# Attention and expert block on one core: normalising the head outputs without transposing them, and row maxima by transposing VectorE reductions

## What is computed

```python
s = jnp.einsum('bthd,bshd->bhts', q, k) * scale
logits = DEG * jnp.log(jnp.abs(s) + 1e-30) + log_G[:, :, :, None] - log_G[:, :, None, :]   # DEG = 2
logits = jnp.where(mask, logits, -jnp.inf)                        # causal
m = jax.lax.stop_gradient(jnp.max(logits, axis=-1, keepdims=True))
a = jnp.exp(logits - m)
num = jnp.einsum('bhts,bshd->bthd', a, v)
den = jnp.sum(a, axis=-1).transpose(0, 2, 1)
y = num / (den[..., None] + 1e-06)
mu = jnp.mean(y, axis=-1, keepdims=True)
var = jnp.mean((y - mu) ** 2, axis=-1, keepdims=True)
y = (y - mu) / jnp.sqrt(var + 1e-09) * ln_w
return y.reshape(B, T, hq * d) @ w_proj
```

## Time and profile before

| | |
|---|---|
| time, median of three runs | 1030.43 us (1028.33 to 1031.97) |
| profiled execution, first to last instruction | 1027.0 us |
| busy: PE, DVE, ACT, POOL | 959.8, 876.1, 676.7, 631.0 us |
| attention pairs | the first scores begin at 148 us, the last nt copy is at 992 us |

### The profile page before, as it was taken

One profiled execution on the slowest core, in us unless ns is written; L12 is line 12 of the kernel. 1 busy time (PEld: TensorE's weight loads), 2 busy tenths in 40 slices (PEclk: granted clock), 3 DMA queues, 4 the chain that ended last, 5 costly groups with the idle time before them and its releaser, 6 DMA issues.

```text
span 1027.0 us, 23345 instructions
## 1 busy us (share of the span) xinstructions
PE 959.8 (93%) x8871; PEld 707.3 (69%) x8871; DVE 876.1 (85%) x1730; ACT 676.7 (66%) x1077; POOL 631.0 (61%) x593
## 2 busy tenths in 40 slices
PE   3999989899999999999999999999999999999964
PEld 2675567567676767687777677777768677768643
DVE  5668738899999998998999898988898989898892
ACT  1243447676766677868778867787876877886731
POOL 0320438889898966666658566748575856766711
PEclk9999999999999999999999999999999999999996
DMA  9401105443434354454444344435434535433540
GB/s 262 102 1 47 51 12 146 106 107 95 108 98 101 101 135 111 104 135 119 104 126 124 97 126 107 119 82 143 104 98 118 127 85 133 112 97 96 147 125 22
DMA packets 77952, 108.66 MB, mean 106 GB/s; under 512 B 15853, under 2 KB 46445, under 8 KB 77712
## 3 DMA queue, kind: packets, MB, share of 16 engines
q1 hardware_dynamic: 72768, 104.50, 39.3%
q0 software_dynamic: 5072, 2.67, 1.9%
HBM read 31.61 MB, written 11.36 MB: 42 GB/s over the span
## 4 chain that ended last, share of the span: by engine, by line
PE 72%; DVE 16%; POOL 4%; issue 4%; ACT 2%; DMA 1%; SPq 1%; POOLq 0%; DVEq 0%; ACTq 0%
PE PS L545 19%; PE PS L737 19%; PE PS L770 18%; PE PS L540 6%; DVE PS L1336 3%; PE PS L588 3%; PE PS L591 3%; PE PS L598 3%; DVE U L1336 2%; DVE PS L1329 2%; POOL U L1439 1%; DVE SM L1361 1%; DVE U L1300 1%; POOL xe_d L1471 1%; PE PS L561 1%
## 5 line engine op out<-in xcount | busy, mean ns | idle before, releaser
L737 PE MATMUL PS<-Qt,Kt 64*128 64x256 f32 (+1 forms) x2560 | 276.8, 366 | 13.5 <-POOL Qt L1442 9.4
L737 PEld LDWEIGHTS PS<-Qt,Kt 64*128 64x128 f32 x2560 | 229.7, 188 | 52.9 <-POOL Qt L1442 11.3
L916 ACT ACTIVATE U<-PS 128x1024 f32<-128x1024 f32 x144 | 140.9, 1023 | 62.5 <-PE PS L737 58.7
L1439 POOL TENSOR_TENSOR U<-U,consts 128x512 f32<-128x512 f32 x96 | 126.2, 1315 | 45.5 <-DMA U<-U 45.5
L770 PE MATMUL PS<-U 128*64 128x256 f32 (+1 forms) x1344 | 139.8, 349 | 0.2 <-ACT U L912 0.2
L1461 POOL TENSOR_SCALAR_AFFINE_SELECT U<-U 128x256 f32<-128x256 f32 x128 | 61.8, 560 | 102.9 <-ACT U L841 102.6
L770 PEld LDWEIGHTS PS<-U 128*64 128x64 f32 x1344 | 93.2, 137 | 40.2 <-issue 5.7
L1507 POOL TENSOR_TENSOR U<-U,SM 128x1024 f32<-128x1024 f32 x32 | 72.2, 2257 | 68.0 <-DVE SM L1356 68.0
L1336 DVE SCALAR_TENSOR_TENSOR PS<-U,ES,PS 128x512 f32<-128x512 f32 x144 | 108.4, 752 | 4.7
L1300 DVE SCALAR_TENSOR_TENSOR U<-PS,U 128x768 f32<-128x768 f32 x96 | 88.3, 952 | 26.2 <-PE PS L737 23.9
L841 ACT ACTIVATE U<-U,negG 128x256 f32<-128x256 f32 (+1 forms) x256 | 98.7, 455 | 5.6 <-DMA U<-H_d 5.3
(11 more groups left out here) (177 smaller groups left out, 1890.7 us busy)
## 6 DMA issues: line engine op xcount, KB each, us to landing
G<-U SPq DMA_DIRECT2D x512, 64.0 KB
U<-U SPq DMA_DIRECT2D x192, 128.0 KB
U<-H_d SPq DMA_DIRECT2D x32, 512.0 KB
Kt<-Kt SPq DMA_DIRECT2D x32, 256.0 KB, 3.9
U<-in_w SPq DMA_DIRECT2D x21, 256.0 KB
acc<-in_x SPq DMA_DIRECT2D x4, 512.0 KB, 5.5
ye_d<-G SPq DMA_DIRECT2D x4, 512.0 KB, 8.0
U<-ye_d SPq DMA_DIRECT2D x4, 512.0 KB, 5.3
```

Of the source, the lines that this page charges most:

```text
L737: mm = te.matmul(bank[:, 256 * n:256 * n + 256 - lo], Kt[u % 2][(ki + hd) % 2][rows, 128 * j:128 * j + 128], Qt[p % 2][m // 2][rows, 256 * ...
L916: s.activation(A[n % NA], PS[:, first:first + 1024], ACT.Square, scale=0.125, bias=GUARD).then_inc(a_so, 1)
L1439: g.tensor_tensor(sw, sw, sinT[:, cols], ALU.mult).then_inc(made, 1)
```

## The change

It does two things, and moves what hangs on them.

Row maxima: once `RUN` is written, DVE itself reduces it with `apply_transpose`: from 128 x 512 it makes 16 columns of `MR`, in each group of 32 partitions the maximum over the partitions of that group. SP moves 16 columns (2 KB a DMA) rather than 512, into `MF`, still 16 DMAs a pair. `fold` on `G`, the four `max` flips and the reduction at L1255 go. `RUN` is one buffer rather than two.

Norm: the values stay as they are, channels on partitions. ACT copies the sums directly into `Y` (four buffers rather than two) and squares the whole into `SQ` (`sq`). Once for two pairs, TensorE multiplies a 128 x 32 selection matrix with `SQ` (`ss`: eight matmuls with 256 columns, each into 32 PSUM partitions), which gives the sums of squares and the squared denominators; DVE (`scales`) transposes them in 32 x 32 blocks, forms the factors of both pairs in 14 small operations on 32 to 64 columns, and transposes back. SP stores the factors in DRAM (`roots`, one DMA of 128 KB) and reads them back spread over partitions (`spread`, four DMAs that each write 64 partitions x 4 KB, one for each head of each pair), into `SQ`. POOL multiplies `Y` by it (`norm`, once a pair, 128 x 1024), and `wp` takes `Y` as it is. All `y` and `fin` flips, the copies L871 and L877, `sums`, `variance`, `root`, `n1` and `n2` go. The jobs get new ticks; `wp` moves from 59.3 to 62, its addition from 49.5 and 54.2 to 63.6 and 64.

Two constants, GUARD and CLAMP, are changed, and the selection matrix is added to the constants. Core of the diff:

```diff
-GUARD = 1e-15
-CLAMP = 60.0
+GUARD = 1e-8
+CLAMP = 30.0
+FLOOR = 1e-17
...
-PE_AT = [(34.43, "max", 0), (19.9, "y", 0), (23.88, "y", 1), (51.85, "fin", 0), (58.3, "fin", 1), (59.31, "wp", 0),
-         (59.72, "wp", 1), (1.41, "xe", 0), (10.46, "up", 0), (14.9, "up", 1), (15.75, "up", 2), (32.48, "up", 3),
+PE_AT = [(33, "ss", 0), (62, "wp", 0), (62.1, "wp", 1), (1.41, "xe", 0), (10.46, "up", 0), (14.9, "up", 1), (15.75, "up", 2), (32.48, "up", 3),
...
-          (10.31, "decay", 3), (23.4, "y", 0), (31.69, "y", 1), (54.54, "fin", 0), (55.63, "fin", 1),
-          (43.3, "ysq", 0), (8.58, "xe", 0), (21.82, "up", 0), (23.77, "up", 1), (25.18, "up", 2), (44.23, "up", 3),
+          (10.31, "decay", 3), (36, "sq", 0), (29, "sq", 1), (8.58, "xe", 0), (21.82, "up", 0), (23.77, "up", 1), (25.18, "up", 2), (44.23, "up", 3),
...
-DVE_AT = [(23.72, "fold", 0), (27.44, "max", 0), (49.5, "wp", 0), (54.22, "wp", 1), (27.9, "sum", 0),
-          (32.03, "var", 0), (34, "root", 0), (34.29, "root", 1), (37.4, "root", 2), (28.36, "up", 4),
+DVE_AT = [(33, "scales", 0), (63.6, "wp", 0), (64, "wp", 1), (28.36, "up", 4),
...
-           (3.66, "vs", 3), (30.16, "n1", 0), (38.34, "n2", 0), (-21.4, "k", 0), (-15.9, "k", 1), (-15.66, "q", 0),
+           (3.66, "vs", 3), (67, "norm", 0), (51, "norm", 1), (-21.4, "k", 0), (-15.9, "k", 1), (-15.66, "q", 0),
...
+         (-25.73, "swapq", 0), (-11.27, "keys", 0), (-14.53, "row", 0), (-10.6, "weights", 0), (4.79, "weights", 1), (32, "roots", 0), (34.5, "spread", 0)]
...
-        RUN = [take(512) for _ in range(2)]
+        RUN = take(512)
         D = [take(384) for _ in range(3)]
-        Y = [take(1024) for _ in range(2)]
-        YT = [take(1024) for _ in range(2)]
-        NT, VS0 = take(512), take(384)
+        Y = [take(1024) for _ in range(4)]
+        ZT, RT, RR, MF = (take(256) for _ in range(4))
+        VS0 = take(384)
...
             def rows(p, w):
 
-                m = ORDER[w]
-                sp.wait_ge(s_zy, 64)
-                sp.wait_ge(v_mx, 16 * p + MAXOPS[w + 1])
-                if p:
-                    sp.wait_ge(v_fold, 2 * p)
+                m, u, c = ORDER[w], p // 2, 16 * (4 * (p % 4) + w)
+                sp.wait_ge(v_red, 4 * p + w + 1)
+                if u > 1:
+                    sp.wait_ge(v_m, u - 1)
                 for j in range(4):
-                    sy.dma_start(G[32 * m:32 * m + 32, 512 * j:512 * j + 512],
-                                 RUN[w % 2][32 * j:32 * j + 32]).then_inc(s_g[w % 2], 16)
+                    o = 128 * (u % 2) + 64 * (p % 2) + 16 * j
+                    sy.dma_start(MF[32 * m:32 * m + 32, o:o + 16],
+                                 MR[32 * j:32 * j + 32, c:c + 16]).then_inc(s_g[u % 2], 16)
+
+            def store_roots(u):
+
+                sp.wait_ge(v_rr, u + 1)
+                if u > 1:
+                    sp.wait_ge(s_rb[0], 32 * (u - 1))
+                    sp.wait_ge(s_rb[1], 32 * (u - 1))
+                sy.dma_start(R_d[128 * (u % 2):128 * (u % 2) + 128], RR).then_inc(s_rd, 16)
+
+            def spread_roots(u):
+
+                sp.wait_ge(s_rd, 16 * (u + 1))
+                sp.wait_ge(p_ss, u + 1)
+                for i in range(2):
+                    for hd in range(2):
+                        sy.dma_start(SQ[i][64 * hd:64 * hd + 64, :].rearrange("p (m q) -> p m q", m=4),
+                                     R_v[u % 2, 2 * i + hd].partition_broadcast(64)).then_inc(s_rb[i], 16)
...
-                elif kind == "max":
-                    p = job[1]
+                elif kind == "ss":
+                    u = job[1]
                     pb = bank_of(job)
-                    pe.wait_ge(v_fold, 2 * p + 2)
-                    for k2 in range(2):
-                        for hd in range(2):
-                            q, o = 2 * k2 + hd, 256 * hd + 128 * k2
-                            tr = flip(pb[:, 128 * q:128 * q + 128], F[:, o:o + 128])
-                    tr.then_inc(p_max, 1)
-                elif kind == "y":
-                    p, i = job[1:]
-                    pb = bank_of(job)
-                    pe.wait_ge(a_nt, 2 * p + i + 1)
-                    for q in range(4):
-                        tr = flip(pb[:, 128 * q:128 * q + 128], NT[:, 128 * q:128 * q + 128])
-                    tr.then_inc(p_y, 1)
-                elif kind == "fin":
-                    p, half = job[1:]
-                    pb = bank_of(job)
-                    pe.wait_ge(g_n2, p + 1)
-                    for q in range(4):
-                        o = 512 * half + 128 * q
-                        tr = flip(pb[:, 128 * q:128 * q + 128], Y[p % 2][:, o:o + 128])
-                    tr.then_inc(p_fin, 1)
+                    pe.wait_ge(a_sq, 2 * u + 2)
+                    pe.wait_ge(s_ct, 16)
+                    for i in range(2):
+                        for m in range(4):
+                            mm = te.matmul(pb[32 * m:32 * m + 32, 0:256], K_[:, C_SEL + 32 * i:C_SEL + 32 * i + 32],
+                                           SQ[i][:, 256 * m:256 * m + 256], start=i == 0, stop=i == 1)
+                    mm.then_inc(p_ss, 1)
                 elif kind == "wp":
                     u, half = job[1:]
                     h = 2 * u % 8
                     pb = bank_of(job)
-                    pe.wait_ge(a_yt, 4 * u + 4)
+                    pe.wait_ge(g_n, 2 * u + 2)
                     for q in range(4):
                         o = 512 * half + 128 * q
                         for pp in range(2):
-                            mm = product(pb[:, 128 * q:128 * q + 128], YT[pp][:, o:o + 128],
+                            mm = product(pb[:, 128 * q:128 * q + 128], Y[(2 * u + pp) % 4][:, o:o + 128],
...
-                elif kind == "y":
-                    p, i = job[1:]
-                    ac.wait_ge(p_y, 2 * p + i + 1)
-                    if p > 1:
-                        ac.wait_ge(p_fin, 2 * (p - 2) + 2)
-                    s.activation(Y[p % 2].rearrange("p (m w c) -> p w m c", m=2, w=2)[:, i],
-                                 P[BANK[job]].rearrange("p (m c) -> p m c", m=2), ACT.Copy).then_inc(a_y, 1)
-                elif kind == "fin":
-                    p, half = job[1:]
-                    ac.wait_ge(p_fin, 2 * p + half + 1)
-                    ac.wait_ge(v_f, 15 * p + 3)
-                    s.activation(YT[p % 2][:, 512 * half:512 * half + 512], P[BANK[job]][:, :], ACT.Copy).then_inc(a_yt, 1)
...
-                    ac.wait_ge(p_y, 2 * p + i)
-                    s.activation(NT, P[4][:, :], ACT.Copy).then_inc(a_nt, 1)
+                    if p > 3:
+                        ac.wait_ge(p_wp, 2 * (p // 2 - 1))
+                    s.activation(Y[p % 4].rearrange("p (m w c) -> p w m c", m=2, w=2)[:, i],
+                                 P[4][:, :].rearrange("p (m c) -> p m c", m=2), ACT.Copy).then_inc(a_nt, 1)
...
-                elif kind == "ysq":
-                    ac.wait_ge(g_n1, p + 1)
-                    ac.wait_ge(p_wp, 2 * (p // 2))
-                    s.activation(YT[p % 2][:, 0:1008].rearrange("p (n d) -> p n d", d=63),
-                                 Y[p % 2].rearrange("p (n d) -> p n d", d=64)[:, :, 0:63], ACT.Square).then_inc(a_ysq, 1)
+                elif kind == "sq":
+                    ac.wait_ge(a_nt, 2 * p + 2)
+                    ac.wait_ge(s_zy, 64)
+                    if p > 1:
+                        ac.wait_ge(p_ss, p // 2)
+                        ac.wait_ge(g_n, p - 1)
+                    s.activation(SQ[p % 2][:, :], Y[p % 4], ACT.Square, scale=0.125, bias=FLOOR).then_inc(a_sq, 1)
...
-                if un > 1 and i == m:
-                    ve.wait_ge(*collected(un - 2))
+                if i == m:
+                    ve.wait_ge(v_red, un)
                 if m == 0:
                     a4 = A[s % NA].rearrange("p (a n t) -> p a n t", a=2, n=4)
-                    v.tensor_tensor(RUN[un % 2].rearrange("p (a n t) -> p a n t", a=2, n=2), a4[:, :, 0:2], a4[:, :, 0:3:2],
+                    v.tensor_tensor(RUN.rearrange("p (a n t) -> p a n t", a=2, n=2), a4[:, :, 0:2], a4[:, :, 0:3:2],
                                     ALU.max).then_inc(v_mx, 1)
+                    fold(un)
...
+                if i == m:
+                    fold(un)
+
+            def fold(un):
+
+                p, w = divmod(un, 4)
+                u, c = p // 2, 16 * (un % 16)
+                if u > 1:
+                    ve.wait_ge(s_g[u % 2], 512 * (u // 2))
+                ve.wait_ge(v_mx, 16 * p + MAXOPS[w + 1])
+                v.tensor_reduce(MR[:, c:c + 16], RUN.rearrange("p (b r) -> p b r", r=32), AX, ALU.max,
+                                apply_transpose=True).then_inc(v_red, 1)
...
+            def scales(u):
+
+                ve.wait_ge(s_g[u % 2], 512 * (u // 2 + 1))
+                v.tensor_reduce(M_.rearrange("p (a c) -> p a c", a=2),
```

(50 more changed lines are left out.)

128 lines of the change are left out of this document (47 added, 81 removed).

## The result

The changed kernel takes 1135.72 us (median of four runs, 1125.85 to 1147.34), the kernel before 1029.49 us (four runs): a ratio of 1.0998, 95% interval 1.0959 to 1.1038, or 103 us. The slowest of the four (1147.34) ran in a slower state and is left out of the ratio; the other three are 1132 us on average. The forecast was 975 us, faster. The sign is wrong, and the time lies 124 us beyond the range; even rival (a), 1056, falls 80 us short.

What follows compares the result with a forecast made beforehand. PE was taken to bound the kernel late, PE, DVE and POOL together early, a dependent chain at the end. Savings of 39.6, 12.6 and 3.5 us, together 55.7, took the span from 1027.0 to 971.3, median 975 us; range 955 to 992.

Steps and rivals of the forecast that it cites:

- rival (a): The spread lands late, POOL stands in norm, and PE waits for queries in each of 15 groups; 1056 us, chance 0.11.
- rival (c): A transposing reduction on DVE costs 1.37 us, so late DVE needs more time than PE; 1022 us, chance 0.07.
- (d): The matmuls of ss on PE run one after another, so PE saves nothing late; 1021 us, chance 0.03.
- The range's lower end: 955 us, from PE's 1.9 us a pair, an early stage of 2.2 us a pair and 7 at the end.
- late, only PE's work counts: From 400 us on PE alone sets the pace; 22 pairs at 1.8 us saved give 39.6 us.
- The burst: DVE's `scales`, once for two pairs: 14 small operations at 2.9 us, 4.1 with transposes and reduction, 2.05 a pair.
- So roots is hidden: On SP the store waits for DVE's factors at no cost, since the queries' swap behind it waits for PE's projection anyway.
- the 1.6 us to spare for q1: POOL's second rotation of the queries, behind norm, ends at 964.2 us; PE's scores want it at 965.84.
- The bank is costed at nothing: PE's wait for the PSUM bank of ss, which DVE reads: put at nothing, 16 us in all at most.
- Busy time: PE per late pair: flips removed save 2.5 us, ss adds 0.7; net 1.8 less, from 26.7 to 24.9 us.
- The end: From the last copy of values to the last wp: 24.9 us before, 21.4 after, 3.5 less.
- `scales` less its reduction: A DVE step at the kernel's end, put at 3.8 us; with copy, square, ss and gaps 7.1 us.

## Why the prediction was wrong

**The prices that decide the rivals were right.** Transposing reduction 0.711 for 0.69 us, which settles rival (c) against it, ss 1.0 us for 16 records, which settles (d), norm 2.41 for 2.6, the number of SP issues. The transposing reduction takes hardly more than the plain one (711 ns beside the 686 of L1255). The Trainium skill (Vector Engine (DVE) Microarchitecture Reference, The reshape front-end and per-opcode configuration) states one element per cycle and lane for the transposing front end; the trace agrees (256 columns more cost 711 - 446 = 265 ns). Two prices were low: the 14 small operations take 4.3 us a group and not 2.9, and L1324, which the sum left as it was, takes 1172 ns and not 811. The range's lower end does not follow from its terms either: 22 x 1.9, 7.9 x 2.2 and 7 are 66 us, which gives 964 and not 955.

**The step that failed first: "late, only PE's work counts".** It was read from PE's 562.98 of 566 us. That PE was full said that every other engine handed over in time, in this order, and nothing of how little was needed for one to be late: DVE stood at 508 of 566 us, but its idle tenth did not lie where the new work came. The sum set amounts against amounts and so took the maxima half as a gain; alone it lost 16 us, and of 34 us less of reductions in its line 18.5 were the kernel's. PE was full because nothing was late, and I took that for slack elsewhere.

**The burst.** I put `scales` at 4.1 us for two pairs into DVE's sum, where it vanished below PE's. It is one piece of 6.2 us in the group shown (4.6 at the end, where POOL is idle), and what stands behind it decides: the odd pair's diagonals, 3.11 us of PE's idle time there. Measured as a whole, 52 us. The place was in the table (33 ticks, with the diagonals at 38.9), and the prediction even used it to say that the factors are ready early.

**"So roots is hidden", and the 1.6 us to spare for q1.** Store and spread cost 44 us, but not by the way of rival (a). SP waited for the factors 63.2 us in 16 waits (5.1 at most); in the group shown the swap was not held by that, since SP stood idle again from 288.69 to 291.83. POOL waited for the spread before a norm 12.7 us in ten waits, apart from the last one at the end.

PE did wait for q1, 16.6 us in five waits, 16.4 of it between 192 and 400 us, but without store and spread it waits 23.6, and without the small operations 5.26 us in the same place. The time from swap to q1 is 17.6 us with and without the burst (291.83 to 309.48, 285.26 to 302.90). What changed in that group is PE's own work ahead of these scores: from the start of the queries' projection PE came to them after 21.7 us before (276.89 to 298.55, with flips and wp between) and is ready after 15.1 now (289.23 to 304.28), while q1 is through after 21.5 and 20.3. The saving on PE was in part a wait for POOL there; no run tests that by itself.

The 44 us are in what I had not asked: who stands behind the spread on SP (rows, decay row, keys, weights), PE's waits for keys and weights, 33 us where the kernel before has 0.3; and in the end of the kernel. The packets, which I had only as bytes, are about a third of it: 12,480 packets fewer are 16 us. One transfer of the spread lands in 5.7 us (median), where I took 5 for two.

**"The bank is costed at nothing".** PE waits for it in eight places (2.6 us at 282.91, 3.7 at most, 16.8 in all), near the 16 us I gave as the most. It was the one cover that I had priced, and by that price.

**Busy time.** PE's was forecast to fall by 1.8 us a pair and did not: the flips went, and the rest ran at a lower clock, 25 ns on each of 2560 score matmuls. In the late window this is 1.8 of the 5.7 us by which a pair is longer than forecast; 3.9 are idle time. Where the clock of that window is 0.99, without factors, store and spread, busy time did fall, to 25.3 us.

**The end.** 30.2 us from the last copy of values (1087.45) to the last wp (1117.64), not 21.4. `scales` starts at 1099.68, 11 us after the square: DVE works on until then, on the last maxima, eight additions of the experts' outputs (L1411) and two of wp (L1259), and the twelve last row transfers, issued one after another (8.60 us from 1088.39), would not have let it start before 1097. The forecast's "`scales` less its reduction" left this step out. Then it takes 4.6 us, store and spread are near the forecast (8.7 us for 9.6), and both norms stand behind the spread (4.63 us for 2.6).

The parts by the runs: maxima half +16; the norm on squares without factors, store and spread -10 (1.0062 beside 1.0158); store and spread +44; small operations +52. They add up to the 103 us by construction, since each is the difference of two neighbours in one order of taking away. Another order could give other parts: the packets gave 16 us at one place and 29 at another.

## What to carry to other kernels

When an engine is full, ask of each new piece of work not how much it is but which instruction stands behind it on its queue and when that one is wanted; add its time to the path unless the trace shows idle time there. The chain here passes through four in-order queues (DVE, SP, POOL, ACT), and no move took it out of the way: twelve runs moved work, and each was slower than the kernel it started from, while each run that only took small operations, bytes, packets or columns out of the new work gained. Less work is no gain by itself, though: the change and its maxima half both left every engine less busy, and both lost. In this kernel a spread was cheaper with one long piece for each partition.

## What the runs showed of the hardware

The first operation of a unit's maxima, L1324, takes 1172 ns on average, where the same operation before takes 811 (and 813 with the maxima half alone), 23 us over 64 of them. It reads two operands from SBUF, and in the group above it takes 1.91 us at 304.00, beside POOL's norm of 302.98 to 305.33; quiet it takes 0.76. The Trainium skill (SBUF — State Buffer, Who interferes with whom) states that a VectorE instruction with two SBUF inputs contends with a GpSimd instruction that reads SBUF. The trace agrees, and here VectorE comes later and waits for nearly all of the norm: 305.33 less 304.00 and 0.76 more is 2.09 us for 1.91 measured. The norm is not alone in it: L1324 takes 1.93 us at 293.82 beside POOL's L1456 and 1.86 at 300.22 beside its rotation. The longer mean belongs to the norm's half of the change (1083 ns without factors, store and spread), but no run says which of POOL's operations makes it. The small operations of `scales` show the same (L1363, 1.22 us beside a rotation, 0.27 at the end). Nothing of this was in the sum.

A transposing reduction of 128x512 float32 takes 711 ns, one of 256 columns 446; a transpose of 256 columns out of PSUM 0.44 us. A transfer costs SP 0.6 to 0.7 us to issue, whether it carries 2 KB (L482, 2.41 us for four) or 256 KB (L499, 2.65 for four).
